# Pre-norm block on one core: the output projection with z stationary, the output bias added by GpSimd

## The chip, the cores and the metric

One core of one Trainium2 chip runs the whole program. The metric is the device time of one execution in microseconds (us). Engines go by the profile's names: PE (TensorE), DVE (VectorE), ACT (ScalarE), POOL (GpSimd), SP (the engine that issues transfers).

## What is computed

`x` is 16 sequences of 512 rows of 128 values, fp32. An attention with 16 heads of 64 and a feed-forward part with quantised operands are each added to it:

```python
h = layernorm(x)
q, k, v = h@Qs + Qbs, h@Ks + Kbs, h@Vs + Vbs      # per head
z = softmax(causal(q @ k.T / 8)) @ v
x1 = x + einsum('bqhk,hkd->bqd', z, O) + Ob       # what the change touches
g = layernorm(x1)
out = x1 + fp4(silu(fp4(g)@fp4(w_gate).T) * (fp4(g)@fp4(w_up).T)) @ fp4(w_down).T
```

`fp4` scales blocks of 16 values and rounds them to a grid of eight magnitudes.

## The kernel before

Work goes in slots. A slot `t` (from -34 to 127) takes one step of every stage of a software pipeline, each for a pair of heads or, in the feed-forward part, a duo of 2 x 128 rows. A stage has a lead: `SCORE` 22 means that slot t does the scores of pair t + 22. Eight pairs are a sequence, so the pattern repeats every eight slots. There is no scheduler. Each engine has a function `do(s)` whose calls at its end are its order within a slot, and engines wait for one another by semaphores.

PE's order in a slot is: scores (line 255, 16 records), weighted values (L271, 40 records), gate and up (L339, L341; every fourth slot), the projection of keys (L217 to L219), `x_turn` (L307), the down projection `down` (L372, 12 records), the output projection `oproj` (L386), the projection of queries, `xq_turn` (L328), the projection of values, `fin` (L316), `hq_turn` (L354, L360). An fp32 product of the program shows as two matmul records, a turning (a transpose through PE) as one.

The output projection of a pair is one matmul with the weights `wo_sb` stationary and `zT` (two heads' z, turned, 512 rows wide) moving. It sums over eight pairs in the PSUM bank `acc`, so the result stands turned, features on partitions:

```python
nc.tensor.matmul(acc[:, :], wo_sb[:, po % NPAIR, :], zT[:, po % 2, :], start=(po % NPAIR == 0),
                 stop=(po % NPAIR == NPAIR - 1)).then_inc(o_done, 1)
```

Once in eight slots the sum leaves `acc`. In slots t = 5 mod 8 ACT's `take_attn` (L701) copies it to `attnT` with the bias `bo_col`. In slots t = 6 mod 8, PE's `fin` turns the four 128x128 blocks back, and DVE's `residual` (L930), late in its slot, adds them to the rows of x that a transfer has put in `x1`. `f_stats1` (L942) and `f_stats2` (L951) follow on DVE and `f_root` (L505, L507) on POOL. One slot on, DVE's `f_bias` (L958) and ACT's `f_norm` (L756) use the result.

POOL's order is `hq7`, `hq8`, `normalise(0)`, `hq9`, `normalise(1)`, `xq7` to `xq9`, `x_root`, `hq_units`, `normalise(2)`, `xq_units`, `f_root`. `hq7` (L524), `hq8` (L530) and `hq9` (L538) are 704 wide, in one slot of four each. `normalise` is L517.

On ACT, `take_attn` stands between `tanh(1)` and `move(0, 3)`. `move` issues the transfers from `squares` or `w_in` to `pT`, which PE's weighted values read two slots after the DVE transposes. Two of ACT's eight moves, the second 256-wide exponential, and the copies of k (L658) and q (L650) to SBUF come behind `take_attn`.

PE's PSUM targets come from a ring of seven banks (`take_bank`). A bank is waited for until what was put in it seven allocations before has been taken. `acc` is the eighth bank. In slots t = 3 mod 8 the second `up` result lies seven allocations before the second bank of the next slot's scores. So scores of slots t = 4 mod 8 wait for DVE's second `swiglu2` (L1022).

## Time and profile before

| | |
|---|---|
| three runs | 1258.76, 1259.02, 1259.97 us; median 1259.02 |
| profiled execution, first to last instruction (span) | 1256.5 us |
| PE busy | 1186.2 us (94%), 9610 matmul records |
| weight loads (PEld) | 843.2 us (67%) |
| DVE busy | 1130.9 us (90%) |
| ACT busy | 997.1 us (79%) |
| POOL busy | 858.5 us (68%) |
| granted PE clock | 0.986 of full |

The profile gives no other time for its own execution than the span, which is 2.5 us under the median of the runs. Matmuls are pipelined: a record's duration includes its way through the array, so the ends of successive records, not durations, tell what each adds. An idle time is printed in brackets, behind it what ended it.

### The profile page before, as it was taken

To read this page: it belongs to the slowest core of one execution; us is meant where nothing else is said; L and a number is where in the kernel's file an instruction comes from. 1 tells how busy PE (TensorE), PEld (TensorE's weight loads), DVE (VectorE), ACT (ScalarE), POOL (GpSimd) and SP (SyncE) were. 2 spreads that over 40 slices of the span, in tenths; PEclk is the share of its full clock that TensorE was granted. 3 is DMA by queue.
4 is the path that set the end of the run, shared out by engine and by line. 5 is a ranking of instruction groups with operands and counts; after the bars stand their busy time and mean duration, and the time that the engine had idled before them with its cause. 6 is when DMAs were issued, how large, how long until landed. Compare 5 with 4: busy or idle time off the path is not lost. (4 is left out here: it accounts for less than half of the span.)

```text
span 1256.5 us, 35752 instructions
## 1 busy us (share of the span) xinstructions
PE 1186.2 (94%) x9610; PEld 843.2 (67%) x9610; DVE 1130.9 (90%) x3771; ACT 997.1 (79%) x2894; POOL 858.5 (68%) x1379
## 2 busy tenths in 40 slices
PE   5877999999999999999999999999999999999864
PEld 3655676777777677777777677767777777777643
DVE  5899889999999998999999899999999999999867
ACT  6767888888889788888988888798888879888521
POOL 3443557867777786767778676777767677777753
PEclk9999999999999999999999999999999999999887
DMA  4554666666565566656666665556665556656610
GB/s 102 156 135 120 172 156 159 166 155 159 148 159 153 154 163 157 156 143 160 154 161 159 158 157 152 149 158 161 157 164 156 148 149 156 163 149 163 171 30 13
DMA packets 132520, 185.43 MB, mean 148 GB/s; under 512 B 40328, under 2 KB 66784, under 8 KB 132320
## 3 DMA queue, kind: packets, MB, share of 16 engines
q1 hardware_dynamic: 82128, 98.93, 30.5%
q10 hardware_dynamic: 50192, 84.21, 25.9%
q8 instruction: 79, 1.29, 0.5%
q14 instruction: 121, 0.99, 0.3%
HBM read 11.04 MB, written 4.19 MB: 12 GB/s over the span
## 5 line engine op out<-in xcount | busy, mean ns | idle before, releaser
L517 POOL TENSOR_SCALAR sc<-sc,rinv 128x512 f32<-128x512 f32 (+3 forms) x1024 | 536.5, 541 | 337.6 <-DVE rinv L882 334.4
L636 ACT ACTIVATE sc<-sc,negmax 128x512 f32<-128x512 f32 (+3 forms) x1024 | 563.0, 552 | 173.4 <-DVE negmax L871 124.3
L871 DVE CUSTOM_DVE_ANT_0 sc<-bank,mask 128x512 f32<-128x512 f32 (+3 forms) x1024 | 434.8, 485 | 50.4 <-issue 40.4
L255 PE MATMUL bank<-k_sb,q_sb 64*128 64x512 f32 (+3 forms) x2048 | 316.0, 444 | 12.2 <-ACT k_sb L658 5.5
L271 PE MATMUL bank<-pT,v 128*64 128x128 f32 x5120 | 309.9, 276 | 8.0 <-DMA pT<-w_in 6.3
L271 PEld LDWEIGHTS bank<-pT,v 128*64 128x64 f32 x5120 | 279.1, 137 | 51.0 <-issue 46.2
L255 PEld LDWEIGHTS bank<-k_sb,q_sb 64*128 64x128 f32 x2048 | 168.4, 186 | 148.0 <-issue 101.4
L894 DVE STREAM_TRANSPOSE squares<-sc 128x1024 f32<-128x1024 f32 (+1 forms) x192 | 194.7, 1043 | 0.8
L894 DVE STREAM_TRANSPOSE w_in<-sc 128x1024 f32<-128x1024 f32 (+1 forms) x192 | 192.0, 1038 | 2.1 <-POOL sc L517 1.9
L636 ACT ACTIVATION_READ_ACCUMULATOR sc<-sc,negmax 128x1 f32 x1024 | 193.8, 189 | 0.0
L386 PE MATMUL bank<-zT,wo_sb 128*128 128x512 f32 x256 | 131.5, 595 | 0.0
L217 PE MATMUL bank<-x_hi,wq_hi 128*128 128x512 f32 x128 | 99.9, 780 | 0.0
L671 ACT ACTIVATE zT<-bank,bcol 128x512 f32<-128x512 f32 x128 | 86.7, 677 | 15.3 <-PE bank L271 7.9
L650 ACT ACTIVATE q_sb<-bank,bcol 128x512 f32<-128x512 f32 x128 | 86.6, 677 | 1.9 <-PE bank L219 1.8
L658 ACT ACTIVATE k_sb<-bank,bcol 128x512 f32<-128x512 f32 x128 | 86.2, 674 | 0.9 <-PE bank L219 0.9
L871 DVE DVE_READ_ACCUMULATOR2_ANT negmax<- 128x1 f32 x1024 | 84.5, 82 | 0.0
L217 PE MATMUL bank<-x_hi,wk_hi 128*128 128x512 f32 x128 | 68.9, 538 | 11.6 <-DVE negmax L871 10.1
L682 ACT ACTIVATE v<-bank 128x512 f32<-128x512 f32 x128 | 75.1, 592 | 0.0
L882 DVE RECIPROCAL rinv<-rsum 128x2 f32<-128x2 f32 (+1 forms) x384 | 56.0, 153 | 14.2 <-ACT sc L636 13.7
L577 POOL TENSOR_TENSOR hq_y<-hh,hq_rec 128x704 f32<-128x704 f32 x32 | 44.6, 1395 | 13.1 <-DVE hq_rec L1054 13.1
L372 PEld LDWEIGHTS bank<-wdT,hqT 128*128 128x128 f32 (+1 forms) x384 | 49.7, 198 | 5.4 <-ACT hqT L730 2.2
L217 PE MATMUL bank<-wv_hi,x_hi 128*128 128x512 f32 x128 | 53.0, 414 | 0.0
(123 smaller groups left out, 1668.1 us busy)
## 6 DMA issues: line engine op xcount, KB each, us to landing
pT<-squares SPq DMA_DIRECT2D x512, 80.0 KB, 2.5
pT<-squares ACTq DMA_DIRECT2D x512, 80.0 KB, 2.3
pT<-w_in SPq DMA_DIRECT2D x512, 80.0 KB, 2.4
pT<-w_in ACTq DMA_DIRECT2D x512, 80.0 KB, 2.4
x_in<-ttn_normalized_resid_pre SPq DMA_DIRECT2D x16, 256.0 KB, 3.3
x<-ttn_normalized_resid_pre SPq DMA_DIRECT2D x16, 256.0 KB, 3.4
out_x<-y_out SPq DMA_DIRECT2D x32, 128.0 KB, 2.7
w_in<-in_L_attn_Ks SPq DMA_DIRECT2D x2, 256.0 KB, 5.2
```

Of the source, the lines that this page charges most:

```text
L217: nc.tensor.matmul(dst, st[0], mv[0], start=True, stop=False)
L255: last = nc.tensor.matmul(to[a][:, at:at + m], q_sb[rows, hs % 2, P * i:P * i + P], k_sb[rows, hs % 2, 0:m], start=True, stop=True)
L271: last = nc.tensor.matmul(to[DH * a:DH * a + DH, P * i:P * i + P], v1[:, pv // NPAIR % 2, j, 2 * (pv % NPAIR) + a, :], pT[:, pv % 2, :, at ...
L386: nc.tensor.matmul(acc[:, :], wo_sb[:, po % NPAIR, :], zT[:, po % 2, :], start=(po % NPAIR == 0), stop=(po % NPAIR == NPAIR - 1)).then_inc ...
L517: last = nc.gpsimd.tensor_scalar(p, p, rinv[:, h % 2, a, i:i + 1], 1.0, ALU.mult, ALU.mult)
L636: last = nc.scalar.activation(p, p, ACT.Exp, scale=-1.0, bias=negmax[:, he % 2, a, i:i + 1], accum_out=rsum[:, he % 2, a, i:i + 1])
L650: nc.scalar.activation(q_sb[:, pj % 2, :], bank_at["q", pj][:, :], ACT.Identity, bias=bcol[:, r:r + 1], scale=DH ** -0.5).then_inc(q_taken, 1)
L658: nc.scalar.activation(k_sb[:, pj % 2, :], bank_at["k", pj][:, :], ACT.Identity, bias=bcol[:, r:r + 1]).then_inc(k_taken, 1)
L671: nc.scalar.activation(zT[:, pv % 2, :], bank_at["z", pv][:, :], ACT.Identity, bias=bcol[:, r:r + 1]).then_inc(zt_taken, 1)
L682: nc.scalar.activation(v1[:, vb % 2, j, NH // 2 * n:NH // 2 * (n + 1), :], bank_at["v", vn][:, :].rearrange("p (h k) -> p h k", k=DH), ACT ...
L871: last = nc.vector.tensor_tensor_reduce(out=sc[:, h % 2, a, AT[i]:AT[i] + m], in0=bank_at[f"S{c}{a}", h][:, at:at + m], in1=mask[:, SEQ - ...
L894: nc.vector.transpose(squares[ht % 2][:, :, :, :].rearrange("p c (a b) q -> p a b c q", a=2)[:, :, lo // P:hi // P, :, :], sc[:, ht % 2, : ...
```

## The change

The operands of the output projection change places. `zT` is now stationary, in four blocks of 128 rows, and `wo_sb` of the pair moves, so `acc` comes out with rows on partitions and needs no turning. `take_attn`, `attnT` and `fin` go. The bias is loaded as `bo_row`, the same 128 values on every partition, and POOL's new `res_bias` adds it to the residual rows in `x1` at the end of its slots t = 1 mod 8. DVE's `residual` reads `acc` and `x1`, and stands behind `row_max(0, 0)`, early in the slot. PE's first output projection of a sequence now waits for that `residual` (`x1_done`) and no longer for `take_attn`.

```diff
-        bo_col = sb("bo_col", [P, 1])
+        bo_row = sb("bo_row", [P, D])
-        attnT = sb("attnT", [P, SEQ])
...
-                def fin():
-                    if bf is None:
-                        return
-                    pe.wait_ge(attn_taken, bf + 1)
-                    to = take_bank("fin", bf, x1_done, bf + 1)
-                    for j in range(NT):
-                        last = nc.tensor.transpose(to[:, P * j:P * j + P], attnT[:, P * j:P * j + P], ident[:, :])
-                    last.then_inc(fin_done, 1)
...
-                    if po % NPAIR == 0:
-                        if po // NPAIR > 0:
-                            pe.wait_ge(attn_taken, po // NPAIR)
-                    nc.tensor.matmul(acc[:, :], wo_sb[:, po % NPAIR, :], zT[:, po % 2, :], start=(po % NPAIR == 0),
-                                     stop=(po % NPAIR == NPAIR - 1)).then_inc(o_done, 1)
+                    if po % NPAIR == 0 and po > 0:
+                        pe.wait_ge(x1_done, po // NPAIR)
+                    for j in range(NT):
+                        last = nc.tensor.matmul(acc[:, P * j:P * j + P], zT[:, po % 2, P * j:P * j + P], wo_sb[:, po % NPAIR, :],
+                                                start=(po % NPAIR == 0 and j == 0),
+                                                stop=(po % NPAIR == NPAIR - 1 and j == NT - 1))
+                    last.then_inc(o_done, 1)
...
-                    sp.dma_start(bo_col[:, :], bo.rearrange("(d o) -> d o", o=1)).then_inc(ld_o, 16)
+                    sp.dma_start(bo_row[:, :], bo.rearrange("(o d) -> o d", o=1).to_broadcast([P, D])).then_inc(ld_o, 16)
...
+                br = s.due(RES - 2, NB, NPAIR)
...
+                def res_bias():
+                    if br is None:
+                        return
+                    if br == 0:
+                        pool.wait_ge(ld_o, 32)
+                    pool.wait_ge(res_loaded[br % 3], 16 * (br // 3 + 1))
+                    nc.gpsimd.tensor_tensor(x1[:, br % 3, :, :], x1[:, br % 3, :, :],
+                                            bo_row[:, :].rearrange("p (o d) -> p o d", o=1).to_broadcast([P, NT, D]),
+                                            ALU.add).then_inc(res_biased, 1)
...
                 f_root()
+                res_bias()
...
-                def take_attn():
-                    if bo is None:
-                        return
-                    act.wait_ge(o_done, NPAIR * (bo + 1))
-                    if bo > 0:
-                        act.wait_ge(fin_done, bo)
-                    nc.scalar.activation(attnT[:, :], acc[:, :], ACT.Identity, bias=bo_col[:, 0:1]).then_inc(attn_taken, 1)
...
-                take_attn()
...
-                    dve.wait_ge(fin_done, bf + 1)
-                    dve.wait_ge(res_loaded[bf % 3], 16 * (bf // 3 + 1))
-                    nc.vector.tensor_tensor(x1[:, bf % 3, :, :], bank_at["fin", bf][:, :].rearrange("p (j d) -> p j d", d=D),
+                    dve.wait_ge(o_done, NPAIR * (bf + 1))
+                    dve.wait_ge(res_biased, bf + 1)
+                    nc.vector.tensor_tensor(x1[:, bf % 3, :, :], acc[:, :].rearrange("p (j d) -> p j d", d=D),
                                             x1[:, bf % 3, :, :], ALU.add).then_inc(x1_done, 1)
...
                 row_max(0, 0)
+                residual()
                 row_max(1, 0)
...
-                residual()
                 f_stats1()
```

PE, the second half of a slot t = 6 mod 8, before: output projection (L386), queries, turning of xq, values, the four turnings back (L316).

```order
L386 MATMUL bank<-zT,wo_sb 128x512
L217 MATMUL bank<-x_hi,wq_hi 128x512
L218 MATMUL bank<-x_lo,wq_hi 128x512
L219 MATMUL bank<-x_hi,wq_lo 128x512
L328 MATMUL bank<-ident,xq 128x128 x2
L217 MATMUL bank<-wv_hi,x_hi 128x512
L218 MATMUL bank<-wv_lo,x_hi 128x512
L219 MATMUL bank<-wv_hi,x_lo 128x512
L316 MATMUL bank<-ident,attnT 128x128 x4
L255 MATMUL bank<-k_sb,q_sb 128x512 x2
```

The same place in the change, up to the next slot's scores; the output projection has line 376:

```order
L376 MATMUL bank<-wo_sb,zT 128x128 x4
L216 MATMUL bank<-x_hi,wq_hi 128x512
L217 MATMUL bank<-x_lo,wq_hi 128x512
L218 MATMUL bank<-x_hi,wq_lo 128x512
L318 MATMUL bank<-ident,xq 128x128 x2
L216 MATMUL bank<-wv_hi,x_hi 128x512
L217 MATMUL bank<-wv_lo,x_hi 128x512
L218 MATMUL bank<-wv_hi,x_lo 128x512
L254 MATMUL bank<-k_sb,q_sb 128x512 x2
```

One matmul has become four (records double in both), and the four turnings have gone.

DVE, the slot t = 6 mod 8, before: row maxima, three transposes, then the residual (L930).

```order
L871 ISA sc,negmax<-bank,mask 128x384
L871 ISA negmax 128x1
L871 ISA sc,negmax<-bank,mask 128x128
L871 ISA negmax 128x1
L882 RECIPROCAL rinv<-rsum 128x2
L894 STREAM_TRANSPOSE w_in<-sc 128x2x4x4x32 x2
L894 STREAM_TRANSPOSE w_in<-sc 128x2x2x4x32
L882 RECIPROCAL rinv<-rsum 128x4
L930 TENSOR_TENSOR x<-bank,x 128x512
L942 BN_STATS fstat<-x 128x6 x2
L882 RECIPROCAL rinv<-rsum 128x2
L951 BN_AGGR fmv<-fstat 128x2 x2
```

In the change, around the residual (L924):

```order
L865 ISA sc,negmax<-bank,mask 128x512
L865 ISA negmax 128x1
L865 ISA sc,negmax<-bank,mask 128x512
L865 ISA negmax 128x1
L924 TENSOR_TENSOR x<-bank,x 128x512
L865 ISA sc,negmax<-bank,mask 128x384
L865 ISA negmax 128x1
L865 ISA sc,negmax<-bank,mask 128x128
```

The residual has moved ahead of six of the eight row maxima and of the transposes.

POOL, end of a slot t = 1 mod 8 and start of the next, in the change (`res_bias` is L578, `hq7` is L516, `normalise` is L509):

```order
L543 TENSOR_TENSOR xq_y<-xq_y,xq_e 128x256
L551 TENSOR_TENSOR xq<-xq_y,xq_scale 128x256
L509 TENSOR_SCALAR sc<-sc,rinv 128x256 x2
L578 TENSOR_TENSOR x<-x,bo_row 128x512
L516 TENSOR_TENSOR hq_y<-hq_y,hq_e 128x704
L509 TENSOR_SCALAR sc<-sc,rinv 128x512 x2
L509 TENSOR_SCALAR sc<-sc,rinv 128x384
```

Before, `hq7` followed directly on the two 256-wide rows; the bias now stands between them.

## Rows read from the trace of the kernel before

**Rows 1.** Windows of eight slots: length, then busy (count) per engine, PE clock, DMA

```profile
609.87:682.60 72.73, 72.73 (x601) 51.96 (x601) 67.62 (x232) 61.43 (x181) 53.94 (x86) 1.00 0.61 158
...
sum 948.55, PE 945.77 PEld 674.56 DVE 881.00 ACT 802.10 POOL 696.75; mean PE 72.75 PEld 51.89 DVE 67.77 ACT 61.70 POOL 53.60
```

**Rows 2.** Windows of single slots t = 6 mod 8; the sum is over 14 such slots

```profile
564.80:573.94 9.14, 8.55 (x75) 6.18 (x74) 6.90 (x24) 8.34 (x25) 8.81 (x15) 1.00 0.75 205
...
638.16:646.66 8.50, 8.50 (x75) 6.14 (x74) 6.61 (x23) 7.72 (x23) 7.88 (x14) 1.00 0.71 186
...
sum 121.83, PE 119.46 PEld 85.73 DVE 97.62 ACT 109.55 POOL 113.77; mean PE 8.53 PEld 6.12 DVE 6.97 ACT 7.82 POOL 8.13
```

**Rows 3.** Timeline, PE, slot 45: start, duration, operation, count

```profile
634.25 0.39 PE L219 MATMUL bank<-x_hi,wk_lo 128*128 128x512 f32 x1
634.48 1.50 PE L372 MATMUL bank<-wdT,hqT 128*128 128x128 f32 x12
635.82 1.02 PE L386 MATMUL bank<-zT,wo_sb 128*128 128x512 f32 x2
```

**Rows 4.** Timeline, PE, slot 46, before and at the turning back

```profile
645.89 0.40 PE L219 MATMUL bank<-wv_hi,x_lo 128*128 128x512 f32 x1
646.13 0.60 PE L316 MATMUL bank<-ident,attnT 128*128 128x128 f32 x4
```

**Rows 5.** Groups by shape, TensorE weight loads of the down projection

```profile
L372 PEld LDWEIGHTS bank<-wdT,hqT 128*128 128x128 f32 x256 | 37.4, 199 | 5.4 <-ACT hqT L730 2.2 <-issue 0.7
```

**Rows 6.** Timeline, ACT, slot 37

```profile
563.63 0.68 ACT L701 ACTIVATE attnT<-bank,bo_col 128x512 f32<-128x512 f32 x1
564.22 0.51 ACT L636 ACTIVATE sc<-sc,negmax 128x256 f32<-128x256 f32 x1
```

**Rows 7.** Timeline, PE, slot 38

```profile
567.81 2.40 PE L271 MATMUL bank<-pT,v 128*64 128x128 f32 x40 [0.59 <-DMA pT<-w_in]
...
570.95 1.02 PE L386 MATMUL bank<-zT,wo_sb 128*128 128x512 f32 x2
```

**Rows 8.** Groups by shape, POOL

```profile
L524 POOL TENSOR_TENSOR hq_y<-hq_y,hq_e 128x704 f32<-128x704 f32 x31 | 52.6, 1697 | 0.5 <-DVE hq_e L1067 0.5
...
L577 POOL TENSOR_TENSOR hq_y<-hh,hq_rec 128x704 f32<-128x704 f32 x32 | 44.6, 1395 | 13.1 <-DVE hq_rec L1054 13.1
...
L551 POOL TENSOR_TENSOR xq_y<-xq_y,xq_e 128x256 f32<-128x256 f32 x31 | 22.7, 731 | 2.4
```

**Rows 9.** Timeline, POOL, slots 42 and 43

```profile
606.62 1.71 POOL L524 TENSOR_TENSOR hq_y<-hq_y,hq_e 128x704 f32<-128x704 f32 x1
...
609.92 2.74 POOL L517 TENSOR_SCALAR sc<-sc,rinv 128x384 f32<-128x384 f32 x6 [0.25 <-DVE rinv L882]
...
613.13 0.71 POOL L507 TENSOR_TENSOR frstd<-fvar,half_pow 128x2 f32<-128x2 f32 x1
...
613.81 1.68 POOL L530 TENSOR_TENSOR hq_y<-hq_y,hq_e 128x704 f32<-128x704 f32 x1
```

**Rows 10.** Timeline, DVE, slot 43

```profile
614.95 0.56 DVE L958 SCALAR_TENSOR_TENSOR fbias<-fmv,frstd 128x2 f32<-128x2 f32 x1
...
619.89 0.52 DVE L1022 SCALAR_TENSOR_TENSOR hh<-ha,bank 128x352 f32<-128x352 f32 x1
```

**Rows 11.** Timeline, PE, scores of slot 44

```profile
621.16 1.13 PE L255 MATMUL bank<-k_sb,q_sb 64*128 64x512 f32 x4
```

**Rows 12.** Timeline, DVE, end of slot 67

```profile
839.68 0.52 DVE L1022 SCALAR_TENSOR_TENSOR hh<-ha,bank 128x352 f32<-128x352 f32 x1
```

**Rows 13.** Timeline, PE, scores of slot 68

```profile
840.41 1.77 PE L255 MATMUL bank<-k_sb,q_sb 64*128 64x512 f32 x8
```

**Rows 14.** Timeline, all engines, slot 110

```profile
1207.45 0.69 DVE L930 TENSOR_TENSOR x<-bank,x 128x512 f32<-128x512 f32 x1 [3.27 <-PE bank L316]
...
1209.25 0.23 POOL L505 TENSOR_SCALAR fvar<-fmv 128x2 f32<-128x2 f32 x1 [1.13 <-DVE fmv L951]
```

**Rows 15.** Timeline, DVE, slot 38: the second 512-wide row maximum

```profile
566.73 0.69 DVE L871 CUSTOM_DVE_ANT_0 sc<-bank,mask 128x512 f32<-128x512 f32 x1
```

More of the change, by code:

```diff
@@ L145, in preln_block_kernel @@
         p_moved = [[sem(f"p_moved{n}{c}") for c in range(4)] for n in range(2)]
-        z_done, zt_taken, o_done, attn_taken = sem("z_done"), sem("zt_taken"), sem("o_done"), sem("attn_taken")
-        fin_done, x1_done = sem("fin_done"), sem("x1_done")
+        z_done, zt_taken, o_done = sem("z_done"), sem("zt_taken"), sem("o_done")
+        res_biased, x1_done = sem("res_biased"), sem("x1_done")
         f_stat, f_stats, f_rstd, f_normed = sem("f_stat"), sem("f_stats"), sem("f_rstd"), sem("f_normed")
@@ L224, in do @@
                 hs, pj, pv, po = (s.due(v, PAIRS) for v in (SCORE, PROJ, PV, OPROJ))
-                bx, bf = s.due(XT, NB, NPAIR), s.due(FIN, NB, NPAIR)
+                bx = s.due(XT, NB, NPAIR)
                 fx, fu, fh, fy = (s.due_duo(v) for v in (FXT, FUP, FHT, FY))
@@ L405, in do @@
                 vproj()
-                fin()
                 hq_turn()
@@ L625, in do @@
                 he, hm, pj, pv = (s.due(v, PAIRS) for v in (SCORE, MOVE, PROJ, PV))
-                bx, bo = s.due(XT, NB, NPAIR), s.due(FIN + 1, NB, NPAIR)
+                bx = s.due(XT, NB, NPAIR)
                 fc, fx, fu, fh = (s.due_duo(v) for v in (FNORM, FXT, FUP, FHT))
```

## The prediction

> **What bounds the kernel now.** I read the busy table, then windows of eight slots, then single slots, then the timelines of the places that the change touches. In a window of eight slots PE is busy 72.73 of 72.73 us, and over 13 such windows 945.77 of 948.55 us, while DVE has 881.00, ACT 802.10 and POOL 696.75 [rows 1]. Since durations of matmul records overlap, I also compared the ends of successive blocks: outside a few places each block adds the same time in every slot. So from slot -10 to slot 103 PE's stream sets the time, and what PE no longer does is gained nearly whole. Before that (the first 130 us or so) DVE and ACT set it, with the weights to prepare, and in the last 75 us PE waits for chains through DVE, POOL and ACT.
>
> The few places are mostly slots t = 6 mod 8. Undisturbed they take 8.50 us; slot 38 took 9.14 us with PE busy 8.55 [rows 2]. Fourteen of them took 121.83 us. Fourteen times 8.50, less 0.70 for the last, which has no values to project (three matmuls of 0.23), is 118.3, so 3.5 us are lost there, in eight of the fourteen.
>
> **The change, part by part.**
>
> *The products (slower).* The nearest rows are those of the down projection, which already has an activation in 128x128 blocks stationary and a 128x128 weight moving, both fp32. Its 12 records move the end of PE's stream from 634.64 to 635.98, 1.34 us or 0.112 each; the old output projection then moves it to 636.84, 0.86 us [rows 3]. Eight new records are 0.893 us, 0.033 more a slot. If they went like turnings (below, 0.109 each) it would be 0.01; taking twice the surplus for the other end, it is 0.01 to 0.07. Over the 114 slots that PE bounds this makes 3.8 us (1 to 8).
>
> *The turning back (gone).* Four turnings move the end from 646.29 to 646.73, 0.44 us [rows 4]. Fifteen of the sixteen lie in the stretch that PE bounds: -6.6 us. PE's net is -2.8.
>
> *`take_attn` (gone).* It costs ACT 0.59 us of its order, from 563.63 to 564.22 [rows 6], and two moves, a 256-wide exponential and the copies of k and q stand behind it. In slot 38 PE stood 0.59 us for a transfer into `pT` [rows 7]; in other such slots it stood for k or q. The eight losses are 0.19 to 0.64 us each, so 0.59 us earlier covers nearly all of the 3.5 us. I take 3.2, and as ends 0 (something else is as late) and 3.5.
>
> *The wait for `x1_done` (costs nothing).* PE's first output projection of a sequence now waits for `residual`, with everything later on PE queued behind it. `residual` itself finds `acc` complete, since PE's last product of the sequence came before this slot's scores. In slot 38 the second row maximum ends at 567.42 [rows 15]; 0.69 us for the residual make it 568.1, and PE's output projection started at 570.95 [rows 7]; undisturbed slots have 0.6 less. The cover is over 2 us. The six row maxima that it now precedes come 0.7 us later, and the banks that they free are taken over 2 us later still. DVE loses its wait for the turning, which shows as 0.4 us of lateness in the next slot; nothing bound hangs on that.
>
> *The transfer of the bias and the ring.* One broadcast load in place of another, long before use. Without `fin` the ring turns one step less in one slot of eight; the bank waits then equal those of other slots. Both nothing.
>
> *`res_bias` (added).* Its price is unknown: the 256-wide two-operand operation takes 0.73, the 704-wide 1.70, and the 704-wide with a broadcast operand 1.40 [rows 8]. Those are the bounds, 0.73 and 1.70; by width it is 1.28, and with a broadcast operand less, so I take 1.2. It waits for a transfer that was issued two slots before, so for nothing. It stands ahead of `hq7` in the slot after. In slots 42 and 43 `hq7` began at 606.62, and POOL from there on idled only 0.25 us until `hq8` at 613.81 [rows 9]. So `hq8` comes 0.95 us later. This matters through DVE: `f_bias` began at 614.95 and ended at 615.51 [rows 10], where `hq8` ended at 615.49. It was held for as long as `hq8` ran, and in all thirteen such slots of the windows above it ends so. Its other DVE neighbours follow it without a gap up to the second `swiglu2`, which ended at 620.41 [rows 10], and PE's scores of slot 44, whose second bank it frees, began at 621.16 [rows 11]. The cover is 0.75 us, the shift 0.95: a stall of 0.2 on PE. In slots 67 and 68 the cover was 840.41 less 840.20, 0.21 us, and POOL had no idle time before: a stall of 1.0 [rows 12, 13]. The thirteen such slots had 0.21 to 1.05 us of cover and 0 to 0.8 us of idle time on POOL; one by one, with a shift of 1.2 less the idle time, they give 4.3 us. I take 0.3 a sequence, 3.9 us, because a lagging POOL as in slot 67 need not come back; ends 0 and, with 1.70 for `res_bias`, 9.
>
> The Trainium skill, "SBUF — State Buffer", section "Who interferes with whom", speaks against this part of the change: GpSimd and VectorE share a pair of ports, and an operation that has it holds it to its end. The trace agrees, by the two ends at 615.5. By the rule the term stays; were the ports free, the sum would be 3.9 us lower.
>
> *The end.* In slot 110 DVE idles 3.27 us before the residual, for the turning, and POOL then idles 1.13 us for the statistics that follow [rows 14]. With the last product in `acc` at 1204.4 the residual starts some 3 us earlier, POOL becomes what is late next, and 1.1 us are gained for the chain behind it; ends 0 and 2.
>
> Sum: +3.8 - 6.6 - 3.2 + 3.9 - 1.1 = -3.2 us. Against the span, 1256.5 becomes 1253.3; the 2.5 us outside stay, so against the median of 1259.02 I forecast **1255.8 us**. About 0.2% (2.5 us) is what a measurement can tell from no change here, and the forecast lies just past it.
>
> **Rivals.**
>
> *The covers hold* (`res_bias` is under 0.9 us, or POOL runs ahead). For it: ACT and DVE have idle time each slot, and the covers reached 1.05 us. Against it: `f_bias` already ends with `hq8`. It takes the 3.9 away: 1251.9 us.
>
> *PE gains, and POOL gives it back.* The mechanism is the one above, with `res_bias` at 1.70 us: the shift outgrows every cover and costs 9 us. If in addition `pT` is as late as before (its transfers wait for DVE's transposes too, which come 0.7 us later in these slots), the sum is +3.8 - 6.6 + 9 - 1.1 = +5.1: 1264.1 us. It turns to slower once the stalls pass 0.5 us a sequence and ACT's gain is lost. Against it: 256- and 704-wide rows straddle the size, and 1.70 is the far end.
>
> *The weight loads show.* A load of the down projection's kind takes 0.199 us [rows 5]; unhidden before each of eight records it gives 8 x (0.107 + 0.199) = 2.4 against 0.86 us, 1.6 more in 114 slots, 181 us in place of the 3.8: 1433 us. Against it: the down projection's records come every 0.112 us with the same loads, so each is hidden. The Trainium skill, "TensorE: Matmul & The Clock Gate", Part 3, section "The mechanism", has it that a weight load overlaps running matmuls only where the row group differs, and by that these would show. The trace contradicts it for the down projection.
>
> *Nothing much moves*: the gain on ACT is not there, the rest as forecast: 1259.0 us.
>
> **How the numbers follow.** Forecast 0.40; covers hold 0.22; ACT's gain missing 0.23; POOL gives it back 0.13; loads show 0.01; other 0.01. The forecast's own range, 1253.5 to 1258, straddles the 0.2% line at 1256.5: two thirds of it, all of the second case and a little of the third make 0.52 for faster. Same takes the rest of the first and third, 0.36; slower has 0.12. The range is 1251.0 to 1261.0: it reaches from just under the second case to half-way into the fourth, and leaves out under 2 in 10.
>
> **What would show it.** Right: output projection blocks 0.89 us apart; no attnT and no 0.44 us block; windows of slots t = 6 mod 8 near 8.1 us without disturbed ones; `res_bias` 1.1 to 1.3 us; `f_bias` in slots t = 3 mod 8 longer than 0.7 us and PE standing 0.1 to 1 us before the scores after it; the last 55 us 1 us shorter. Wrong: PE waiting at its output projection; records further apart than 0.112; slots t = 6 mod 8 still uneven (then ACT was not the cause); scores of slots t = 4 mod 8 on time (then the covers held).

## The result and the profile after

The changed kernel takes **1253.97 us** (median of 4 runs, 1252.66 to 1255.13), the kernel before beside it 1258.92 (4 runs). The medians differ by 4.95 us, where 3.2 were forecast. The ratio of the runs is 0.9953 with a 95% interval of 0.9938 to 0.9968, which stands for 5.9 us (4.0 to 7.8), so the change is past the 0.2% line. The profiled execution took 1254.1 us, with a span of 1252.4 (before: 1256.5).

The page's table of busy time. PE is as busy as before in more records, ACT has lost the copy, and POOL has gained 23 us, most of them the addition.

```profile
PE 1185.6 (95%) x10314; PEld 903.3 (72%) x10314; DVE 1133.9 (91%) x3771; ACT 990.0 (79%) x2878; POOL 881.1 (70%) x1395
```

Windows of eight slots, which answer to [rows 1] (slots 19 to 26; the sum is over the same 13):

```profile
387.89:460.50 72.61, 72.61 (x645) 55.63 (x644) 67.75 (x230) 60.73 (x178) 55.29 (x88) 1.00 0.61 158
...
sum 944.71, PE 943.36 PEld 721.72 DVE 882.09 ACT 797.98 POOL 714.01; mean PE 72.57 PEld 55.52 DVE 67.85 ACT 61.38 POOL 54.92
```

The clean window is 72.61 us long in place of 72.73, and PE is still busy in all of it: the bound has not moved. The sum fell by 3.8 us, from 948.55 to 944.71.

Windows of the slots t = 6 mod 8, which answer to [rows 2]:

```profile
561.96:570.06 8.10, 8.10 (x76) 6.13 (x75) 6.79 (x21) 5.85 (x20) 7.04 (x11) 1.00 0.66 170
...
sum 112.99, PE 112.80 PEld 85.52 DVE 99.01 ACT 88.28 POOL 102.07; mean PE 8.06 PEld 6.11 DVE 7.07 ACT 6.31 POOL 7.29
```

Slot 38, which took 9.14 us, takes 8.10, and every other takes 8.09 to 8.11 but the first (8.37) and the last, which has no values to project (7.40). The fourteen take 112.99 us instead of 121.83, 8.8 less: 14 x 0.44 = 6.2 for the turnings and some 3 for the uneven ones, less 0.6 for the dearer products.

Timeline of PE in slot 45, which answers to [rows 3]. The eight new records go from the end of L362, 632.92, to that of L376, 633.81:

```profile
631.75 1.17 PE L362 MATMUL bank<-wdT,hqT 128*128 128x128 f32 x9
632.75 1.06 PE L376 MATMUL bank<-wo_sb,zT 128*128 128x128 f32 x8
633.57 0.48 PE L216 MATMUL bank<-x_hi,wq_hi 128*128 128x512 f32 x1
```

That is 0.89 us where the old product took 0.86. The weight loads of these records (group L376 PEld on the page, 1024 loads, mean 192 ns) lie beside the products.

The new operation on POOL, and slots 42 and 43, which answer to [rows 8] and [rows 9]:

```profile
L578 POOL TENSOR_TENSOR x<-x,bo_row 128x512 f32<-128x512 f32 x16 | 20.6, 1286 | 0.0
```

```profile
603.26 1.28 POOL L578 TENSOR_TENSOR x<-x,bo_row 128x512 f32<-128x512 f32 x1
604.49 1.71 POOL L516 TENSOR_TENSOR hq_y<-hq_y,hq_e 128x704 f32<-128x704 f32 x1
606.18 4.10 POOL L509 TENSOR_SCALAR sc<-sc,rinv 128x512 f32<-128x512 f32 x8
...
611.44 1.70 POOL L522 TENSOR_TENSOR hq_y<-hq_y,hq_e 128x704 f32<-128x704 f32 x1
```

The addition takes 1.286 us, 0.09 over what I took. Between it and `hq8` (L522) POOL idles only 0.24 us, 0.09 ahead of `f_root` and 0.15 inside it. On DVE in slot 43, and on PE at the scores of slot 44 (which answer to [rows 10] and [rows 11]):

```profile
611.50 1.65 DVE L952 SCALAR_TENSOR_TENSOR fbias<-fmv,frstd 128x2 f32<-128x2 f32 x1 [0.57 <-POOL frstd L499]
...
617.38 0.52 DVE L1016 SCALAR_TENSOR_TENSOR hh<-ha,bank 128x352 f32<-128x352 f32 x1
```

```profile
618.05 1.42 PE L254 MATMUL bank<-k_sb,q_sb 64*128 64x512 f32 x5 [0.51 <-DVE hh L1016]
```

`f_bias` (L952) ends at 613.15, with `hq8` at 613.14, and is 1.65 us long where it was 0.56. All behind it on DVE is late, and PE stands 0.51 us for the last `swiglu2`. It starts 0.15 us after `swiglu2` has ended (617.90), as in the other slots in which it waits: a cover of 0.15 us is none. That is the chain which was forecast, but it showed in three slots of thirteen only (waits of 0.51, 0.08 and 0.57 us before the scores of slots 44, 68 and 76). The slots t = 3 mod 8, whose windows end with those scores, take 148.44 us in all.

At slot 110, which answers to [rows 14]:

```profile
1199.77 0.69 DVE L924 TENSOR_TENSOR x<-bank,x 128x512 f32<-128x512 f32 x1 [0.27 <-PE bank L376]
```

```profile
1203.41 0.23 POOL L497 TENSOR_SCALAR fvar<-fmv 128x2 f32<-128x2 f32 x1
```

The residual is 7.7 us earlier than in the profile before, `f_root` 5.8 us, where PE's stream ahead of slot 110 is 4.7 us earlier: the 1.1 us that were forecast for the end. They do not reach the time. The chain of waits ends with the last down projection, 12 records of L362 (L372 before), in the kernel before and in this one:

```profile
1252.09:1253.68 1.59, 1.57 (x12) 1.38 (x12) 0.00 (x0) 0.00 (x0) 0.00 (x0) 1.00 0.27 82
```

```profile
1246.67:1249.58 2.91, 2.90 (x12) 2.60 (x12) 0.00 (x0) 0.00 (x0) 0.00 (x0) 0.50 0.15 45
```

In this execution the clock stood at its lower level there (granted 0.50 of full speed, 1.2 GHz) and the same records took 2.91 us in place of 1.59: 1.3 us given back. The twelve records before them in the chain took 2.58 us in place of 2.18, another 0.4. From slot 104 to the end the profiled executions of all fourteen kernels took 88.8 to 92.8 us, without order; that is a part of the scatter of the runs.

### The profile page after: what moved, and what is told of

The parts are those of the page before. It is cut to its first block and busy times, and to the rows that moved or that the text cites. A ratio compares the mean times of both kernels' runs of the same rounds, so it can differ in the third digit from the quotient of the medians.

```text
span 1252.4 us, 37130 instructions
## 1 busy us (share of the span) xinstructions
PE 1185.6 (95%) x10314; PEld 903.3 (72%) x10314; DVE 1133.9 (91%) x3771; ACT 990.0 (79%) x2878; POOL 881.1 (70%) x1395
## 5 line engine op out<-in xcount | busy, mean ns | idle before, releaser
L509 POOL TENSOR_SCALAR sc<-sc,rinv 128x512 f32<-128x512 f32 (+3 forms) x1024 | 539.2, 545 | 311.5 <-DVE rinv L876 308.7
L254 PE MATMUL bank<-k_sb,q_sb 64*128 64x512 f32 (+3 forms) x2048 | 315.3, 444 | 10.7 <-ACT q_sb L653 3.9
L376 PEld LDWEIGHTS bank<-wo_sb,zT 128*128 128x128 f32 x1024 | 131.5, 192 | 10.0 <-issue 0.7
L376 PE MATMUL bank<-wo_sb,zT 128*128 128x128 f32 x1024 | 136.0, 276 | 0.0
L216 PE MATMUL bank<-x_hi,wq_hi 128*128 128x512 f32 x128 | 61.2, 478 | 0.0
L329 PE MATMUL bank<-wgT,xqT 128*128 128x352 f32 x128 | 53.6, 501 | 0.9 <-ACT xqT L705 0.9
L362 PEld LDWEIGHTS bank<-wdT,hqT 128*128 128x128 f32 (+1 forms) x384 | 49.9, 199 | 5.1 <-ACT hqT L725 2.3
```

The lines of the kernel that those rows point to most:

```text
L216: nc.tensor.matmul(dst, st[0], mv[0], start=True, stop=False)
L254: last = nc.tensor.matmul(to[a][:, at:at + m], q_sb[rows, hs % 2, P * i:P * i + P], k_sb[rows, hs % 2, 0:m], start=True, stop=True)
L376: last = nc.tensor.matmul(acc[:, P * j:P * j + P], zT[:, po % 2, P * j:P * j + P], wo_sb[:, po % NPAIR, :], start=(po % NPAIR == 0 and j = ...
L509: last = nc.gpsimd.tensor_scalar(p, p, rinv[:, h % 2, a, i:i + 1], 1.0, ALU.mult, ALU.mult)
```

## The experiments

Times stand beside runs of the kernel before on the same chip, whose medians were 1258.1, 1258.9, 1259.4 and 1260.0 us in the four groups. So the ratio is what is to be compared; for the changed kernel it is 0.9953.

### Was it ScalarE's copy that made slots t = 6 mod 8 uneven?

```
                 tanh(1)
-                take_attn()
                 move(0, 3)
...
                 take_hq()
+                take_attn()
                 x_norm()
```

> The kernel before, with one edit: ScalarE's copy of the attention output stands behind the two copies of hq in its order, instead of ahead of them. Theory (the 3.5 us of uneven stalls in slots t = 6 mod 8 came from that copy standing ahead of the hq copies on ScalarE): every such slot takes about 8.50 us, none more, and the time is about 3 us under the kernel before (1255.5 to 1256.5). Rival (the 3.5 us came from the turning back itself, from the ring of banks or from the transfer of the projection's result): the uneven slots stay at 8.6 to 9.1 us and the time is that of the kernel before within 0.1%.

Measured: 1254.91 us (12 runs) against 1258.11, ratio 0.9969 (0.9959 to 0.9979). Windows of the slots t = 6 mod 8 of this run:

```profile
561.78:570.28 8.50, 8.50 (x74) 6.12 (x73) 6.91 (x24) 7.90 (x24) 8.16 (x14) 1.00 0.75 200
...
sum 118.31, PE 118.31 PEld 85.23 DVE 97.65 ACT 105.80 POOL 110.58; mean PE 8.45 PEld 6.09 DVE 6.97 ACT 7.56 POOL 7.90
```

All thirteen full ones take 8.50 or 8.51 us, and their sum is 3.5 us less than in [rows 2]. The theory holds: moving one ScalarE instruction gives 3.2 us between medians, with nothing of the change made. That is two thirds of what the whole change gives.

The reverse, in the changed kernel:

```
+                def copy_spare():
+                    if bo is None:
+                        return
+                    nc.scalar.activation(spare[:, :].rearrange("p (j d) -> p j d", d=D),
+                                         wo_sb[:, 0:NT, :], ACT.Copy)
...
                 tanh(1)
+                copy_spare()
                 move(0, 3)
```

> The changed kernel, with one ScalarE copy of 128x512 to a spare tile put where the kernel before had its copy of the attention output; nobody waits for it. Theory (ScalarE's load at that place made the stalls of slots t = 6 mod 8): part or all of 3.5 us comes back, in uneven slots t = 6 mod 8, so 1255.5 to 1257.5. Rival (the stalls came from the order of waits, since the copy waited for the attention output, or from the turning back): the slots stay at 8.10 us and the time is that of the changed kernel, 1254.

Measured: 1254.49 us, ratio 0.9973 (0.9960 to 0.9985). The slots stay at 8.09 to 8.12 us but for the first (8.72); in time it can't be told from the changed kernel. The theory fails here and the rival holds: the copy's 0.62 us on ScalarE did not do it. What the spare copy lacks is the wait. In the kernel before, timeline of ACT in slot 45:

```profile
636.88 0.69 ACT L701 ACTIVATE attnT<-bank,bo_col 128x512 f32<-128x512 f32 x1 [0.46 <-PE bank L386]
637.01 0.51 ACTq L771 DMA_DIRECT2D pT<-w_in  x1
...
638.65 0.68 ACT L650 ACTIVATE q_sb<-bank,bcol 128x512 f32<-128x512 f32 x1
```

`take_attn` stood 0.46 us for the last output projection of the same slot (L386), and behind it in ScalarE's order stand two of the transfers into `pT`, issued from 637.01. The idle time itself is not the measure. In slot 37, ahead of the most uneven slot, ACT came to `take_attn` late and did not idle at all ([rows 6]), and yet the transfers went out at the same place:

```profile
563.65 0.52 ACTq L771 DMA_DIRECT2D pT<-w_in  x1
```

In all twelve slots t = 5 mod 8 from 5 to 93 the first of the two is issued 8.03 us after the start of the slot. So I put the wait back too:

```
+                    act.wait_ge(o_done, NPAIR * (bo + 1))
                     nc.scalar.activation(spare[:, :].rearrange("p (j d) -> p j d", d=D),
```

> The run with the added ScalarE copy (x2_act_copy), with one more edit: the copy first waits for the last output projection of the sequence, as the copy of the attention output did in the kernel before; it still writes a spare tile. Theory (in the kernel before it was this wait, 0.46 us in slot 45, as much as the 0.6 us of the copy, that made the copies of k and q late in slots t = 5 mod 8): the copy of q ends about 10.35 us after the start of such a slot, as in the kernel before, in place of 9.55 in x2_act_copy; slots t = 6 mod 8 are uneven again, by 2 to 4 us in all, and the time is 1256 to 1258.5. Rival (the unevenness needed the late residual or the turning back too): slots t = 6 mod 8 stay at 8.10 and the time is that of x2_act_copy, 1254.5.

Measured: 1255.17 us, ratio 0.9968 (0.9954 to 0.9981). Timeline of ACT in slot 45 with the wait, and without it (x2_act_copy):

```profile
633.79 0.64 ACT L705 ACTIVATE spare<-wo_sb 128x512 f32<-128x512 f32 x1 [0.54 <-PE bank L377]
633.93 0.51 ACTq L775 DMA_DIRECT2D pT<-w_in  x1
...
635.57 0.68 ACT L654 ACTIVATE q_sb<-bank,bcol 128x512 f32<-128x512 f32 x1
```

```profile
632.79 1.11 ACTq L774 DMA_DIRECT2D pT<-w_in  x1
...
634.15 0.65 ACTq L774 DMA_DIRECT2D pT<-w_in  x1
...
634.53 0.62 ACT L704 ACTIVATE spare<-wo_sb 128x512 f32<-128x512 f32 x1
...
636.12 0.67 ACT L654 ACTIVATE q_sb<-bank,bcol 128x512 f32<-128x512 f32 x1
```

With the slots' starts (625.86 and 627.25) taken off, the copy of q ends at 10.39 us with the wait and 9.54 without it; the next transfer is issued at 8.07 with it, and in the run without it the two were issued at 5.54 and 6.90. The kernel before has 10.35 and 8.03. So the theory's first part holds: the wait cost 0.85 us on the copies and up to 2.5 us on two transfers. The transfers lose more than the idle time, since ScalarE's issues run ahead of its work: without the wait both go out before the copy that stands ahead of them has begun (634.53). The second part holds only in part, and the time is under the theory's range, nearer to the rival. The sum of the windows of its slots t = 6 mod 8:

```profile
sum 113.89, PE 113.36 PEld 85.89 DVE 101.29 ACT 101.10 POOL 102.93; mean PE 8.10 PEld 6.14 DVE 7.23 ACT 7.22 POOL 7.35
```

Fourteen clean ones would be 13 x 8.10 + 7.40 = 112.7, so 1.2 us are lost, in place of the 3.5 of the kernel before; the changed kernel loses 0.3 by this measure and x2_act_copy 0.65. The lateness is necessary, as the first run shows, but what uses it up is only partly back. In the kernel before PE waited for `pT` in four slots (38, 54, 78 and 86; 0.29 to 0.59 us) and for the copy of k in slots 22 and 30 (0.35 and 0.09 us). Here it waited for `pT` in one of the full slots, 86 (0.41 us), though the transfers are issued at the same times. The traces show how: ahead of those four slots the second of the two transfers took 2.86 to 3.24 us from issue to landing, ahead of the others 2.03 to 2.42. With the wait in the changed kernel it took 2.01 to 2.32, and 2.95 ahead of slot 86. What slowed these transfers stays open.

### What does the bias addition cost?

```
-                br = s.due(RES - 2, NB, NPAIR)
+                br = s.due(12, NB, NPAIR)
```

> The changed kernel, with the bias addition on GpSimd two slots earlier, in slots t = 4 mod 8 instead of t = 6 mod 8 by its stage, where GpSimd's queue has less in it. Theory (its 1.29 us push the quantisation of hq later, which holds VectorE's f_bias, which makes TensorE wait ahead of the scores of slots t = 4 mod 8): the cover ahead of those scores is back at about 1.0 us, the stalls of 0.25 to 0.6 us in them go, and the time is 1.0 to 2.5 us under the changed kernel (1251.5 to 1253). Rival (those stalls have another cause, such as the residual early in VectorE's slot): they stay, and the time is 1254. Second rival (the new place takes as much from another wait): new stalls of about 1.5 us in all in other slots, time 1253.5 to 1255.

Two details of this expectation are wrong. RES - 2 is 15, slots t = 1 mod 8, so the edit puts the addition three slots later, in t = 4 mod 8, two ahead of the residual (x12_slot4_hq8_odd below has the same slip). What was expected of the stalls doesn't rest on it.

Measured: 1251.35 us (6 runs), ratio 0.9936 (0.9919 to 0.9953). Windows of the slots t = 3 mod 8, of the changed kernel and of this one:

```profile
606.16:618.05 11.89, 11.39 (x92) 8.60 (x92) 10.33 (x32) 11.23 (x33) 9.93 (x16) 1.00 0.44 112
...
sum 148.44, PE 147.28 PEld 111.19 DVE 136.52 ACT 140.26 POOL 122.56; mean PE 11.33 PEld 8.55 DVE 10.50 ACT 10.79 POOL 9.43
```

```profile
604.63:615.95 11.32, 11.32 (x92) 8.57 (x92) 10.54 (x33) 10.78 (x31) 9.35 (x16) 1.00 0.52 131
...
sum 146.93, PE 146.93 PEld 111.08 DVE 136.25 ACT 140.30 POOL 120.63; mean PE 11.30 PEld 8.54 DVE 10.48 ACT 10.79 POOL 9.28
```

1.5 us are gone from these slots, and 1.8 from the windows of eight (942.92 against 944.71). In slot 43 `hq8` starts 3.68 us after the slot's start (in six of the thirteen slots of the kernel before it was 3.72 or 3.73), and `f_bias` is 0.70 us long. PE no longer waits for `swiglu2` in any of the thirteen. The 0.23 us that slot 27 takes over the usual 11.32 stay, so they are not the addition's.

The same without the addition:

```
                 f_root()
-                res_bias()
...
-                    dve.wait_ge(res_biased, bf + 1)
+                    dve.wait_ge(res_loaded[bf % 3], 16 * (bf // 3 + 1))
```

> The changed kernel without the bias addition on GpSimd: the bias of the output projection is left out of the result, and the residual waits for the residual rows alone. Theory (the addition costs what its 1.29 us push hq8 and f_bias, up to 2.5 us at the end of the kernel): the same as with the addition in slots t = 4 mod 8, 1250.5 to 1252.5. If the earlier place of the addition still costs something, it is 1 us or more under that one, 1249 to 1250.5. Rival (the addition is free where it is): 1254.

Measured: 1250.98 us (5 runs), ratio 0.9946 (0.9933 to 0.9959). It can't be told from x3_bias_slot4, so in the later slot the addition costs nothing that these runs could show. Its thirteen slots t = 3 mod 8 take 147.76 us, 0.8 more than in x3_bias_slot4: PE never waits for `swiglu2`, but three other slots (19, 27 and 75) are 0.15 to 0.57 us long for other reasons, such as 0.28 us for a copy of k. One execution scatters by that much. By the four traces that keep the addition where it is with the rest untouched on POOL (148.44 to 148.73 in the changed kernel, x2_act_copy, x7_turn_kept and x10_copy_waits) and the five in which it is gone, moved, or cut off from `f_bias` (146.83 to 147.76 in x3_bias_slot4, x5_hq8_later, x8_no_bias, x11_hq8_odd and x12_slot4_hq8_odd) it costs 1.4 us in these slots on the mean, 0.7 to 1.9 between single ones.

And with the cost doubled:

```
+                    nc.gpsimd.tensor_tensor(spare[:, :, :], wo_sb[:, 0:NT, :],
+                                            bo_row[:, :].rearrange("p (o d) -> p o d", o=1)
+                                            .to_broadcast([P, NT, D]), ALU.add)
                     nc.gpsimd.tensor_tensor(x1[:, br % 3, :, :], x1[:, br % 3, :, :],
```

> The changed kernel, with a second equal addition on GpSimd ahead of the bias addition, into a spare tile. Theory (GpSimd's lateness in these slots passes to TensorE one to one once the cover of about 0.43 us is gone): the quantisation of hq ends 1.3 us later, f_bias ends with it, and TensorE waits 0.8 to 0.9 us ahead of the scores in each of 14 slots t = 4 mod 8, 11 to 13 us in all, so 1265 to 1267. Rival (GpSimd is off the path, and the few stalls seen are chance): 1254 to 1256.

Measured: 1265.80 us, ratio 1.0056 (1.0040 to 1.0072). Windows of the slots t = 3 mod 8 and the scores after slot 43:

```profile
538.85:551.07 12.22, 11.44 (x92) 8.53 (x92) 10.58 (x32) 11.63 (x33) 10.25 (x16) 1.00 0.41 110
...
sum 160.53, PE 149.11 PEld 110.38 DVE 139.17 ACT 151.17 POOL 135.08; mean PE 11.47 PEld 8.49 DVE 10.71 ACT 11.63 POOL 10.39
```

```profile
625.51 0.70 PE L255 MATMUL bank<-k_sb,q_sb 64*128 64x512 f32 x2 [0.79 <-DVE hh L1020]
```

These thirteen slots take 12.1 us more than in the changed kernel, and the time is 11.8 us more. Nine of them are 12.22 to 12.28 us long, where the usual slot of the changed kernel has 11.32: the cover is used up, and PE now waits in all thirteen. The theory holds, in the stall of a slot, its sum and the time.

### Is it the ports that `f_bias` waits for?

```
                 hq7()
-                hq8()
                 normalise(0)
+                hq8()
                 hq9()
```

> The changed kernel, with GpSimd's quantisation of hq (hq8) behind the normalisation of tile 0 in its order, instead of ahead of it, so that it no longer runs beside VectorE's f_bias. Theory (f_bias is held by hq8 running beside it): f_bias is short in slots t = 3 mod 8, the cover ahead of the scores of slots t = 4 mod 8 grows by 1.3 us, their stalls go, and unless the later hq8 is waited for by the transposes of hq the time is 1 to 2 us under the changed kernel (1252 to 1253). Rival (f_bias is late because of VectorE's own queue, not because of hq8): the stalls stay, time 1254. If the transposes of hq wait for the later hq8 it is slower than the changed kernel instead, with stalls in slots t = 3 mod 8.

Measured: 1260.59 us (11 runs), ratio 1.0015 (1.0006 to 1.0024): 6.6 us slower than the changed kernel. `f_bias` takes 0.14 to 0.16 us in all thirteen slots t = 3 mod 8 and their excess falls from 1.7 to 0.3 us, as the theory has it, but the third branch of the expectation decides the time, with another place than named. The window of slot 39 (t = 7 mod 8), and PE at its end:

```profile
573.64:585.21 11.57, 11.12 (x89) 8.11 (x88) 11.01 (x43) 10.06 (x29) 8.96 (x14) 1.00 0.55 145
```

```profile
584.40 0.66 PE L344 MATMUL bank<-ident,hq 128*128 128x128 f32 x4 [0.45 <-POOL hq L530]
```

It is 0.67 us longer (10.90 in the changed kernel) since PE waits for `hq9`, and so in twelve of the fourteen such slots (11.56 to 11.85 us; the last two took 10.89 and 10.66). There `normalise(0)` stands waiting for DVE, and `hq8` now stands behind it. So the edit was made for the slots t = 3 mod 8 alone:

```
                 hq7()
-                hq8()
+                if h4 is None or h4 % 2 == 0:
+                    hq8()
                 normalise(0)
+                if h4 is not None and h4 % 2 == 1:
+                    hq8()
```

> The changed kernel, with GpSimd's hq8 behind the normalisation of tile 0 in slots t = 3 mod 8 alone; in slots t = 7 mod 8, where x5_hq8_later lost 0.67 us each, it stays ahead. Theory (f_bias is held by hq8 and that alone makes the stalls of slots t = 3 and 4 mod 8): f_bias takes 0.14 to 0.16 us in the slots t = 3 mod 8, the excess of 1.7 us in them falls under 0.4, slots t = 7 mod 8 stay at 10.89, and the time is 1.2 to 1.7 us under the changed kernel: 1252.0 to 1253.0. Rival (the late hq8 shifts hq9 and the transposes of hq there too): new stalls of 0.3 us or more in slots t = 3 mod 8, 1256 to 1258.

Measured: 1251.65 us (6 runs), ratio 0.9939 (0.9925 to 0.9953). Timelines of DVE and POOL in slot 43, and the sum over the slots t = 3 mod 8:

```profile
609.55 0.16 DVE L955 SCALAR_TENSOR_TENSOR fbias<-fmv,frstd 128x2 f32<-128x2 f32 x1
```

```profile
608.80 0.72 POOL L499 TENSOR_TENSOR frstd<-fvar,half_pow 128x2 f32<-128x2 f32 x1
609.68 1.37 POOL L509 TENSOR_SCALAR sc<-sc,rinv 128x512 f32<-128x512 f32 x2 [0.16 <-DVE rinv L879]
611.01 1.70 POOL L522 TENSOR_TENSOR hq_y<-hq_y,hq_e 128x704 f32<-128x704 f32 x1
```

```profile
sum 146.83, PE 146.83 PEld 111.09 DVE 129.84 ACT 138.94 POOL 131.83; mean PE 11.29 PEld 8.55 DVE 9.99 ACT 10.69 POOL 10.14
```

Its `hq8` comes behind two rows of the normalisation. `f_bias` starts right after `f_root` has ended (609.52), as in the changed kernel, and works on two numbers per partition as before. With POOL idle (its normalisation begins at 609.68) it takes 0.16 us, beside `hq8` 1.65. So the length of `f_bias` is not its own work nor DVE's queue, but that one neighbour. This is what the Trainium skill, "SBUF — State Buffer", section "Who interferes with whom", states of the shared ports, and here it is shown by taking the neighbour away. Medians over the thirteen slots t = 3 mod 8, from the traces:

```
kernel            hq8 starts, us   f_bias, us   sum of the    time, us
                  after the slot                13 windows
before                3.90            0.74        146.5       1258.9
changed               4.44            1.44        148.4       1254.0
x3_bias_slot4         3.68            0.70        147.0       1251.4
x8_no_bias            3.70            0.71        147.8       1251.0
x4_bias_twice         5.63            1.65        160.5       1265.8
x11_hq8_odd           6.44            0.14        146.8       1251.7
x12_slot4_hq8_odd     6.31            0.14        147.5       1251.6
```

Both edits at once (x3_bias_slot4 and x11_hq8_odd):

> Both edits: the bias addition two slots earlier (x3_bias_slot4) and hq8 behind the normalisation of tile 0 in slots t = 3 mod 8 (x11_hq8_odd). Theory (both act on the same stalls, of which 0.23 us were left with the first alone): no more than 0.5 us under x3_bias_slot4, 1250.8 to 1251.6. Rival (each has a cause of its own): the gains add, 1249.5 to 1250.5.

Measured: 1251.61 us (6 runs), ratio 0.9933 (0.9921 to 0.9945). The gains do not add: they are one stall, removed in two ways. (Its own sum of 147.5 has 0.8 us in slot 27 alone.)

### Does the residual have to be early?

```
                 row_max(0, 0)
-                residual()
                 row_max(1, 0)
...
                 hq6()
+                residual()
                 f_stats1()
```

> The changed kernel, with the residual addition on VectorE back at its late place in the slot. It is now the addition that frees the bank of the output projection and starts norm2 on GpSimd. Theory (the early place is needed once the residual reads the bank): norm2 and the quantisation of hq start some 3 us later, and by the covers measured so far TensorE waits about 3 us in each of 15 sequences, 30 to 50 us in all: 1285 to 1305. Rival (there is slack enough behind it): 1254 to 1258.

Measured: 1314.68 us (4 runs), ratio 1.0459 (1.0437 to 1.0480). Slower than the range. The group of the products, and the timeline of PE at slot 38:

```profile
L376 PE MATMUL bank<-wo_sb,zT 128*128 128x128 f32 x1024 | 138.5, 279 | 42.3 <-DVE x L924 42.3
```

```profile
596.33 1.13 PE L376 MATMUL bank<-wo_sb,zT 128*128 128x128 f32 x8 [2.75 <-DVE x L924]
```

42.3 us of PE's idle time are here, 2.75 in slot 38. The wait is that of the next sequence's first product for `x1_done`; I had put it at norm2 and `hq8`. Most of the rest comes behind it: the records after the wait take longer. Windows from before the wait to the next slot:

```profile
593.50:596.30 2.80, 0.08 (x1) 0.00 (x1) 2.77 (x6) 2.56 (x8) 2.32 (x4) 1.00 0.66 167
596.30:597.50 1.20, 1.17 (x9) 1.19 (x10) 0.72 (x5) 0.00 (x0) 1.20 (x4) 1.00 0.32 77
597.50:600.20 2.70, 2.70 (x10) 1.63 (x8) 0.00 (x0) 0.96 (x2) 2.47 (x6) 0.51 0.56 134
```

After 2.8 us in which PE did next to nothing, it had its full clock for 1.2 us and then the lower level (0.51, 1.2 GHz) for 2.7, which makes this slot 1.2 us longer than those without it. Of the fourteen slots t = 6 mod 8, six kept a granted clock of 1.00 and took 10.8 to 11.3 us; eight had 0.86 to 0.91 and took 12.1 to 13.3, together 11.3 us more than at 11.09 each. One of either kind:

```profile
512.32:523.41 11.09, 8.33 (x77) 6.06 (x76) 7.94 (x29) 7.18 (x22) 10.22 (x18) 1.00 0.60 154
587.92:600.17 12.25, 9.50 (x76) 6.74 (x75) 7.95 (x29) 7.39 (x22) 11.38 (x20) 0.89 0.59 151
```

### The two terms of TensorE's stream

```
+                    to = take_bank("more", bf, z_done, 1)
+                    for j in range(NT):
+                        nc.tensor.transpose(to[:, P * j:P * j + P], wo_sb[:, j, :], ident[:, :])
```

> The changed kernel, with four transposes of 128x128 put back on TensorE at the place of the turning back, from data that are ready into a bank that nobody reads. Theory (TensorE's stream is the bound, and each turning costs 0.44 us): 15 x 0.44 = 6.6 us more, so 1260 to 1261.5. Rival (the transposes fit into time in which TensorE waits): 1254 to 1256.

Measured: the profiled execution took 1260.7 us, 6.6 more than that of the changed kernel, and the slots t = 6 mod 8 take 8.54 us where they took 8.10:

```profile
564.72:573.26 8.54, 8.54 (x80) 6.63 (x80) 7.42 (x26) 6.82 (x21) 7.29 (x12) 1.00 0.65 165
...
sum 119.05, PE 118.95 PEld 92.41 DVE 106.27 ACT 94.23 POOL 103.81; mean PE 8.50 PEld 6.60 DVE 7.59 ACT 6.73 POOL 7.41
```

The term is right in the trace. The median of the six runs is 1263.03 us (1260.72 to 1265.26), ratio 1.0038 (1.0024 to 1.0053), and so 2 us over what was expected, and 9.1 over the changed kernel in place of 6.6 (the ratios say 10.7). The profiled execution is the fastest of them, and where the others lose more stays open.

```
-                    for j in range(NT):
-                        last = nc.tensor.matmul(acc[:, P * j:P * j + P], zT[:, po % 2, P * j:P * j + P],
-                                                wo_sb[:, po % NPAIR, :], ...)
-                    last.then_inc(o_done, 1)
+                    nc.tensor.matmul(acc[:, :], wo_sb[:, po % NPAIR, :], zT[:, po % 2, :],
+                                     start=(po % NPAIR == 0), stop=(po % NPAIR == NPAIR - 1)).then_inc(o_done, 1)
```

> The changed kernel, with the output projection of a pair again as one product (the weight stationary, z moving, 512 wide) in place of four with z stationary. The turning back is not put back, so that the attention output is added to the residual rows unturned, which is not what is to be computed. Theory (four products move the end of TensorE's stream 0.034 us more than one, in each of 114 slots that TensorE bounds): 3.9 us under the changed kernel, with slots t = 0 and 4 mod 8 back at 7.83 us in place of 7.88: 1249.5 to 1250.5. Rival (the four products cost more than their own records, by what they delay behind them, up to 0.05 us a slot): 5.7 us under it, 1247.5 to 1249. Second rival (the difference is taken up by waits): 1253 to 1254.

Measured: 1248.81 us (5 runs), ratio 0.9917 (0.9901 to 0.9933). Windows of eight slots, a clean one and the sum of thirteen:

```profile
533.04:605.32 72.28, 72.28 (x597) 51.48 (x596) 68.11 (x234) 61.25 (x180) 54.81 (x87) 1.00 0.60 158
...
sum 940.73, PE 939.55 PEld 668.26 DVE 884.95 ACT 797.34 POOL 712.05; mean PE 72.27 PEld 51.41 DVE 68.07 ACT 61.33 POOL 54.77
```

The clean slots give 72.61 - 72.28 = 0.33 us for eight, 0.041 a slot: 4.7 us over 114 slots. The blocks' own ends give 0.034; where the other 0.007 arise stays open. The medians say 5.2 us and the ratios 4.5. The time is in the range of the first rival; by the windows the price is between it and the theory.

## Why the prediction was right

The forecast was 1255.8 us in a range of 1251.0 to 1261.0, and 1253.97 came: the side, the range and the mechanism were right, and the forecast 1.8 us too high. That it is no more has some luck in it: one term was 0.9 us too low and another 2.5 too high. Term by term:

- **Products**, +3.8 forecast, some +4.7 measured (x13_old_product; 4.5 to 5.2 by the runs). Reading the price off the down projection's records was sound, and 0.893 us per block came out as worked. What was missed is 0.007 us a slot behind the block.
- **Turning back**, -6.6 forecast. With the turnings put back the profiled execution takes 6.6 us more and the slots concerned 6.1, but the medians say 9.1 (x7_turn_kept). The 2.5 us between stay open.
- **`take_attn`**, -3.2 forecast. x1_attn_late shows 3.5 us in the slots concerned, and 3.2 in the median. The size was right, the reason half right. I counted the 0.59 us that the copy takes, and overlooked that it waits for PE, and that this wait holds back two transfers into `pT` until 8.03 us into the slot. Nor did PE stand 0.05 us or more for the copy of q in any of these slots, as the prediction has it, only for that of k. x2_act_copy has the 0.62 us and next to no loss. x10_copy_waits brings the lateness back in full, and 1.2 of the 3.5 us. x1_attn_late shows that the copy's place made the slots uneven; the path is shown as far as the late issue, and why four transfers were then slow is not.
- **`res_bias`**, +3.9 forecast, some +1.4 measured (0.7 to 1.9 in the slots by single traces, 2.3 to 3.0 between medians). This is the step that was mis-sized. The chain is the one told: POOL's addition, `hq8`, `f_bias` held by the ports, `swiglu2`, the scores. The duration was nearly right (1.29 for 1.2), but not what it does to slots that were already late. The 4.3 us were added up one by one, each slot with the lateness it had in that one execution. Nearly half of that sum is two slots, 67 and 75, with about 1.0 us each, because their `hq8` was the latest before (4.62 and 4.61 us after the slot's start). In the changed kernel it came at 4.87 and 5.46 and PE waited 0.08 and 0.57 us. Slot 91, at 4.38 before, came 0.13 us earlier and had no wait in place of 0.75. Where `hq8` had been on time (3.72 or 3.73) it moved by 0.70 to 0.88 us, and a cover of 0.43 us stayed at the median of the thirteen slots (0.75 before). So the lateness of a slot did not carry over from one kernel's execution to the other's with the addition on top.
- **The end**, -1.1 forecast. It is there at slot 110 to the tenth, and was given back in the last products (1.7 us) by the clock of that execution. That it reaches the time is not shown: the ends of the fourteen executions scatter by 4 us.
- **Wait for `x1_done`, transfer, ring**, nothing forecast and nothing seen: no record of L376 in the changed kernel waits. x6_residual_late shows what the cover is worth. With the residual late in the slot it is gone, and PE waits 2.75 us.

With the measured sizes, +4.7 - 6.6 - 3.2 + 1.4 gives -3.7 us, and -4.8 with the end; the medians say -4.95.

Of the rivals, "the covers hold" (1251.9) was nearest in time but wrong in reason: they did not hold in three slots, and `res_bias` is no cheaper than I took it. "POOL gives it back" is a real mechanism with its price too high: x4_bias_twice, with 2.6 us on POOL in place of 1.3, shows it in full, slower than the kernel before. Weight loads did not show: 1024 loads of 192 ns lie beside products that come every 0.112 us. That is against the rule of the Trainium skill that the prediction cites ("TensorE: Matmul & The Clock Gate", Part 3, "The mechanism"). The same section also lets a load be pulled ahead when it goes to a background weight buffer; the trace fits that, though no run here shows where a load goes.

Three versions are 2.3 to 2.6 us under the changed kernel's median (x3_bias_slot4, x11_hq8_odd, x12_slot4_hq8_odd). Their intervals overlap with one another and with that of the changed kernel. What speaks for them is the trace: 1.1 to 2.1 us less in the same thirteen windows of eight slots, and no wait for `swiglu2`. The simplest is the bias addition in slots t = 4 mod 8.

## What to carry to other kernels

An instruction costs its engine its duration and its wait, and both can fall on what stands behind it, transfers that the engine issues among them. The wait may show as no idle time at all when the engine is late anyway, so look at when the transfers behind it are issued, in every such slot. When an operation is added off the critical path, the stalls of single slots can't be forecast from one execution: take the usual slot's shift and cover, count a late slot as chance, and put the operation where its engine idles. And where VectorE's smallest operation is many times longer than its work, look at what GpSimd runs beside it.

## What was not expected of the hardware

- The clock fell after a wait of PE in the midst of the kernel. In slot 38 of x6_residual_late 2.8 us of standing were followed by 1.2 us at full clock and 2.7 us at the lower level, and eight of fourteen such slots had a lower clock (0.86 to 0.91 on their mean); in the other six the clock held. There a wait of PE cost 1.4 us more than it lasted, on the mean of the eight.
- Twelve records of the last down projection took 1.59 us in one execution and 2.91 in another, by the granted clock alone. One profiled execution does not tell differences of 1 us at the end of the kernel.
- A two-input GpSimd addition of 128x512, with one operand repeated for each block of 128, takes 1.286 us. Between the 128x256 (0.73) and the 128x704 (1.70) without repeats a straight line gives 1.28, the prediction's figure by width. So this repeated operand brings no discount, though a repeated operand goes with 1.40 in place of 1.70 us at 128x704, and my 1.2 had the discount wrong.
